# Scores and context of a per-token attention in half tiles, one product to each projection product, with words of q, k and v laid by twos

## What is computed

```python
q = (h @ wq.T + bq).reshape(B, S, H, D)        # H = D = 32; k, v alike
scores = einsum('bshd,bstd->bsht', q, k) / sqrt(D)
probs = softmax(scores, axis=-1)
context = einsum('bsht,bstd->bshd', probs, v).reshape(B, S, E)
x = x + context(layernorm(x))
x = x + ffn(layernorm(x), nf4(w1), nf4(w2), nf4(w3))
```

## Time and profile before

| | us |
|---|---|
| median of 3 runs | 2002.74 |
| lowest, highest | 2000.63, 2002.87 |
| profiled execution: span | 2002.1 |
| PE busy | 1957.2 (98%) |
| DVE busy | 1785.3 (89%) |
| ACT busy | 1456.2 (73%) |
| POOL busy | 1190.3 (59%) |

### The profile page before, as it was taken

How to read it: one execution, slowest core, us unless ns; L and a number is a source line. 1 busy time by engine, 2 the same in 40 slices (tenths; PEclk the granted TensorE clock), 3 DMA queues, 4 the chain that set the end, 5 groups by cost and what they waited for, 6 DMA issues and landing times. The chain is left out here.

```text
span 2002.1 us, 30892 instructions
## 1 busy us (share of the span) xinstructions
PE 1957.2 (98%) x10444; PEld 1072.7 (54%) x10444; DVE 1785.3 (89%) x1789; ACT 1456.2 (73%) x1592; POOL 1190.3 (59%) x714
## 2 busy tenths in 40 slices
PE   6899999999999989999999999999999999999998
PEld 5578777777775434444444444444444444444443
DVE  6788988989878899999999999999999999989982
ACT  7242424233365889989899898998989989898883
...
GB/s 305 90 94 159 143 166 158 136 167 142 127 133 159 220 100 63 42 55 51 52 53 49 55 42 58 47 56 49 43 62 42 63 42 47 58 43 58 38 27 179
DMA packets 253419, 183.77 MB, mean 92 GB/s; under 512 B 177457, under 2 KB 220465, under 8 KB 253361
## 3 DMA queue, kind: packets, MB, share of 16 engines
...
## 5 line engine op out<-in xcount | busy, mean ns | idle before, releaser
L1593 DVE SCALAR_TENSOR_TENSOR bank<-signs,bank 128x1024 f32<-128x1024 int8 (+2 forms) x761 | 926.5, 1217 | 53.9 <-ACT signs L1457 25.9
L1457 ACT ACTIVATE signs<-w_nat,compare_bias 128x1024 int8<-128x1024 f32 (+2 forms) x896 | 959.3, 1133 | 4.2 <-DVE step_part L1591 1.4
L1764 PE MATMUL bank<-x2T_hi,w12T_hi 128*128 128x512 f16 x1376 | 521.5, 379 | 2.1 <-DVE w_nat L1610 1.3
L1765 PE MATMUL bank<-x2T_lo,w12T_hi 128*128 128x512 f16 x1376 | 521.5, 379 | 0.0
L1766 PE MATMUL bank<-x2T_hi,w12T_lo 128*128 128x512 f16 x1376 | 521.5, 379 | 0.0
L985 PE MATMUL bank<-wT_hi,xT_hi 128*128 128x512 f16 x768 | 294.0, 383 | 2.5 <-PEq L324 2.5
L985 PE MATMUL bank<-wT_hi,xT_lo 128*128 128x512 f16 x768 | 294.3, 383 | 0.0
L1791 PE MATMUL bank<-w3T_hi,hT_hi 128*128 128x512 f16 x672 | 255.5, 380 | 9.1 <-DMA w3T_lo<-half 6.3
L1792 PE MATMUL bank<-w3T_lo,hT_hi 128*128 128x512 f16 x672 | 255.4, 380 | 0.0
L1793 PE MATMUL bank<-w3T_hi,hT_lo 128*128 128x512 f16 x672 | 255.2, 380 | 0.0
L1383 POOL TENSOR_TENSOR acc<-acc,hidden 128x512 f32<-128x512 f32 x176 | 221.1, 1271 | 39.4 <-ACT hidden L1506 38.6
(11 more groups left out here) (142 smaller groups left out, 2719.5 us busy)
## 6 DMA issues: line engine op xcount, KB each, us to landing
...
```

The lines of the kernel that those rows point to most:

```text
L1457: nc.scalar.activation(signs[0:rows, ring(v, k), 0:cols], w_nat[0:rows, v % SLOTS, 0:cols], ACT.Sign, scale=COMPARE[SUMMED[k]][0], bias=co ...
L1593: V.scalar_tensor_tensor(to, part, HALF_STEP[SUMMED[k]], before, ALU.mult, ALU.add).then_inc(sign_used, 1)
L1764: nc.tensor.matmul(dst, hi, x2T_hi[:, toks, c], start=c == 0, stop=False)
L1765: nc.tensor.matmul(dst, hi, x2T_lo[:, toks, c], start=False, stop=False)
```

## The change

Four things change together.

1. PE: each of the 32 matmuls of q is followed by one score product, each of the 16 of k's second half by one product of the context's first half, each of the 16 of v's first half by one of its second half.
2. Scores, row maximum, subtraction, exponential, turn, placing and weighing work on halves of 16 positions, a PSUM bank each, with a semaphore count per half. `weigh` and `flip_context` move from the start of the next step (the tail, for tile 14) to the end of the same one. Row maxima and what follows move ahead of q's second evacuation on DVE. The residual moves to the head of POOL's step. ACT's `turn_low2` moves behind the placing of q. The tail's score products keep their places among the early sums, and so do its context products.
3. `qT`, `kT`, `vT` lie as [128, 16, 32, 2]: the turns write two neighbouring words, then step. PE reads kT and vT at every second word.
4. v's dimensions and heads change places: wv's rows are loaded in another order (rows of 4 KB as before), v's bias goes through `qT` and a POOL copy in the first block, and the weighed context and its turn use pairs, too; POOL's add undoes it.

```diff
+                by_dim = w_qkv[2].rearrange("(h t a) e -> t a h e", h=HEADS, a=P // QUAD)
+                for k in range(LOADS):
+                    sp.dma_start(w_raw[2][:, k], by_dim[k]).then_inc(w_in[2][k], 16)
...
+                for m in (2, 0, 1):
+                    to = bias[:, m] if m < 2 else qT[:].rearrange("p t h u -> p (t h u)")
+                    sp.dma_start(to, b_qkv[m].rearrange("(o n) -> o n", o=1).to_broadcast([P, E])).then_inc(bias_in[m // 2], 16)
...
+                pool.wait_ge(bias_in[1], 16)
+                nc.gpsimd.tensor_copy(bias[:, 2].rearrange("p (d h) -> p h d", h=HEADS),
+                                      qT[:].rearrange("p t h u -> p (t h u)").rearrange("p (h d) -> p h d", d=HD)).then_inc(bias_turned, 1)
...
-        kT = sb("kT", [P, QUAD, HEADS])
-        vT = sb("vT", [P, QUAD, HD])
+        kT = sb("kT", [P, QUAD // 2, HEADS, 2])
+        vT = sb("vT", [P, QUAD // 2, HD, 2])
...
+                if end:
+                    residual(n - 2)
...
-                    residual(n - 2)
...
+                rows = x_res[:].rearrange("p (h u d) -> p h u d", u=2, d=HD)
+                nc.gpsimd.tensor_tensor(rows, rows, flipped[:].rearrange("p (h d u) -> p h u d", d=HD, u=2), ALU.add).then_inc(res_done, 1)
...
-                if end:
-                    weigh(n - 2)
                 if attend:
-
                     evacuate(n - 1, 1 - u, it, 2, 1)
+                    turn_v(n)
                 if normalize:
                     norm_stats(dve, n + 1, 1 - u, (n + 1) // 2 + 1 if it is None else it + 2 + u)
-                if end:
-                    flip_context(n - 2)
-                if attend:
-                    turn_v(n)
-                if normalize:
-                    norm_apply(dve, n + 1, 1 - u)
-                look()
                 if end:
                     moments2(n - 2)
...
                 if project:
                     evacuate(n, u, it, 0, 0)
+                if attend:
+                    center(n, 0)
+                if normalize:
+                    norm_apply(dve, n + 1, 1 - u)
+                if attend:
+                    flip_probs(n, 0, end)
+                look()
+                if end:
+                    norm2(n - 2)
+                if attend:
+                    center(n, 1)
+                if project:
                     evacuate(n, u, it, 0, 1)
                 if feed:
                     next(feed)
-                if attend:
-                    center(n)
-                    if feed:
-                        next(feed)
-                if end:
-                    norm2(n - 2)
                 if normalize:
                     split_lo(dve, n + 1, xT_lo[:, 1 - u], xT_hi[:, 1 - u], x_hi_done, x_lo_done)
                 if attend:
-                    flip_probs(n, end)
-                    sum_rows()
-                look()
+                    flip_probs(n, 1, end)
                 if project:
                     dve.wait_ge(evacuated, 6 * n + 2)
                     if not (it is None and n == 0):
                         dve.wait_ge(q_placed, n)
-                    nc.vector.transpose(qT[:].rearrange("p t h -> p h t"),
+                    nc.vector.transpose(qT[:].rearrange("p t h u -> p h t u"),
                                         qkv[:, 0].rearrange("p (h d) -> p h d", d=HD)).then_inc(q_ready, 1)
+                if feed:
...
+                if attend:
+                    sum_rows()
                 look()
                 if project:
                     evacuate(n, u, it, 1, 0)
                 look()
+                if attend:
+                    weigh(n - 1, 0)
                 if project:
                     evacuate(n, u, it, 1, 1)
                     dve.wait_ge(evacuated, 6 * n + 4)
-                    nc.vector.transpose(kT[:].rearrange("p t h -> p h t"),
+                    nc.vector.transpose(kT[:].rearrange("p t h u -> p h t u"),
...
                 look()
                 if project:
                     evacuate(n, u, it, 2, 0)
+                look()
+                if attend:
+                    weigh(n - 1, 1)
+                    flip_context(n - 1)
                 look()
...
-            def weigh(n):
-                dve.wait_ge(context_done, n + 1)
+            def weigh(n, half):
+                part = slice(half * HALF, (half + 1) * HALF)
+                dve.wait_ge(context_done, 2 * n + half + 1)
                 seq.wait(dve)
-                nc.vector.tensor_tensor(probs[:], context, inv_sum[:].unsqueeze(2).to_broadcast([P, QUAD, HD]),
+                nc.vector.tensor_tensor(probs[:].rearrange("p t h -> p (t h)").rearrange("p (d t u) -> p t d u", t=QUAD, u=2)[:, part],
+                                        context[:, part].rearrange("p t (d u) -> p t d u", u=2),
+                                        inv_sum[:, part].unsqueeze(2).unsqueeze(3).to_broadcast([P, HALF, HD // 2, 2]),
                                         ALU.mult).then_inc(ctx_read, 1)
 
             def flip_context(n):
-                dve.wait_ge(ctx_read, n + 1)
-                nc.vector.transpose(flipped[:].rearrange("p (h d) -> p d h", d=HD),
-                                    probs[:].rearrange("p t d -> p d t")).then_inc(ctx_ready, 1)
+                dve.wait_ge(ctx_read, 2 * n + 2)
+                nc.vector.transpose(flipped[:].rearrange("p (h d u) -> p d h u", d=HD, u=2),
+                                    probs[:].rearrange("p t h -> p (t h)").rearrange("p (d t u) -> p d u t", t=QUAD, u=2)).then_inc(ctx_ready, 1)
...
                 dve.wait_ge(evacuated, 6 * n)
-                nc.vector.transpose(vT[:].rearrange("p t d -> p d t"),
-                                    qkv[:, 0].rearrange("p (h d) -> p d h", d=HD)).then_inc(v_ready, 1)
+                nc.vector.transpose(vT[:].rearrange("p t d u -> p d t u"),
+                                    qkv[:, 0].rearrange("p (d h) -> p d h", h=HEADS)).then_inc(v_ready, 1)
...
+            def center(n, half):
+
+                part = slice(half * HALF, (half + 1) * HALF)
+                dve.wait_ge(scores_done, 2 * n + half - 1)
+                seq.mark(nc.vector.tensor_reduce(row_max[:, part], scores[:, part], AX.X, ALU.max))
                 seq.wait(dve)
-                nc.vector.tensor_tensor(probs[:], scores, row_max[:].unsqueeze(2).to_broadcast([P, QUAD, HEADS]),
+                nc.vector.tensor_tensor(probs[:, part], scores[:, part], row_max[:, part].unsqueeze(2).to_broadcast([P, HALF, HEADS]),
                                         ALU.subtract).then_inc(centered, 1)
...
+                if end and half == 0:
                     dve.wait_ge(res_done, n - 1)
...
-                weigh(T - 2)
                 evacuate(T - 1, 1, None, 2, 1)
                 next(feed)
-                flip_context(T - 2)
...
+                center(T, 0)
+                center(T, 1)
+                next(feed)
+                flip_probs(T, 0, True)
+                flip_probs(T, 1, True)
...
+                if attend:
+                    exponential(n, 0)
+                    place_probs(n, 0, end)
...
                 if attend:
-                    exponential(n)
+                    exponential(n, 1)
                 if end:
                     halve2(n - 2)
                     turn_high2(act, n - 2)
                 if attend:
-                    place_probs(n, end)
+                    place_probs(n, 1, end)
                 if feed:
                     next(feed)
-                if end:
-                    turn_low2(act, n - 2)
                 if project:
                     act.wait_ge(q_ready, n + 1)
                     if attend:
...
-                    place(q_diag, qT[:].rearrange("p t h -> p (t h)"), q_placed)
+                    place(q_diag, qT[:].rearrange("p t h u -> p t u h"), q_placed)
+                if end:
+                    turn_low2(act, n - 2)
...
                 if end:
-                    act.wait_ge(context_done, n - 1)
+                    act.wait_ge(context_done, 2 * n + half - 3)
                 else:
                     act.wait_ge(diag_zero, 2)
-                place(p_diag, flipped[:], p_placed)
+                part = slice(half * HALF, (half + 1) * HALF)
+                place(p_diag[:, part], flipped[:].rearrange("p (t u h) -> p t u h", u=2, h=HEADS)[:, half * HALF // 2:(half + 1) * HALF // 2], p_placed)
...
-                    skip = len(passes) if late else len(passes) * 2 // 3 if with_lo else len(passes) // 2
-                    slots = 2 * len(passes) - skip
                     for j, (x, w) in enumerate(passes):
                         ins = nc.tensor.matmul(to, x, w, start=j == 0, stop=j == len(passes) - 1)
                         if j == len(passes) - 1:
                             ins.then_inc(projected, 1)
-                        slot = h * len(passes) + j - skip
-                        if between and slot >= 0:
```

(18 more changed lines are left out.)

82 lines of the change are left out of this document (38 added, 44 removed).

## The result

The changed kernel takes 2016.71 us (median of 7 runs, 2006.62 to 2021.6), the kernel before, on the same chip, 2000.63 (7 runs, 1999.46 to 2004.12). The ratio is **1.0065, 95% interval [1.0047, 1.0083]**: slower by 0.65%, where 1954.3 us had been forecast. The profiled execution took 2010.74 us with a span of 2008.9. It is one of the faster ones: the runs of the changed kernel lie 15 us apart, those of the kernel before 5.

A forecast was written before the change was run, and what follows sets the result against it. The loop was taken to run at PE's rate, with DVE 2.8 us behind. Gains of 27.7 (loop), 8.7 (step 15) and 12.0 (tail) summed to 48.4 us, giving 1954.3 us; range 1950 to 1959 at 0.50, wider 1945 to 1972.

The forecast's parts named there:

- Loop, PE: Tile steps 1 to 14 on PE: 30.64 us a step instead of 32.62, a gain of 27.7 us in all.
- Loop, DVE: DVE in a loop step: halving adds 1.0 us, turns at 1.24 to 1.3 us each save 3.1; 27.8 of 30.6 us busy.
- Loop, the new deadlines: Work on halves in a loop step is ready at least 2 us before PE needs it; SP's loads keep their order.
- Rival 4: Loop: turns not shortened, DVE becomes the bound, PE stalls at half clock, about 2120 us; or products cost more; chance 0.05.
- First steps: Start and step 0: wv's loads move the same bytes in 4 KB rows; effect 0, with -0.5 to +3 us.
- Step 15: Last tile step: no long placing stall, then PE waits for POOL's second diagonal; 34.8 us instead of 43.48, gain 8.7.
- Tail: Stretch up to the feed-forward: no wait for `p_diag`, DVE next to bound; 42 us instead of 53.95, gain 12.0.
- rival 1: Tail: PE's clock stays at half through the 32 score products after idling, 9 us longer, time 1963; chance 0.22.
- rival 2: Only the loop gains; the tail finds other waits and step 15 stalls as before; 1975 us; chance 0.10, whole or part.

The follow-up runs named there:

- both_mended: Changed kernel with each wv load issued as four of 32 rows, and the loop's low-half x2 DMA transpose issued after v's first-half evacuation; 1972.15 us, ratio 0.9854.
- before_wv_by_dim: The kernel before with only the changed kernel's eight wv loads, v's columns then in the wrong order; 2029.07 us, ratio 1.0130.
- wv_four_loads: Changed kernel with each of the eight wv loads issued as four of 32 rows, same rows to same places; 1990.38 us, ratio 0.9929.

## Why the prediction was wrong

*Loop, PE.* Right: 30.64 us a step in eight of 14 of the changed kernel and in all 14 once the meeting of transfers was taken away, in nine kernels; 27.6 for 27.7.

*Loop, DVE.* Right: 1.20 to 1.25 us a turn, and DVE busy 26.1 us a step (364.98 in 14 steps of both_mended) for 27.8. Of the 1.7 too much 1.0 is the start from one tile with 29.87 us, where the 14 steps had 28.9 on average (404.41 in 14). The Trainium skill ("SBUF — State Buffer", Door 1: The DMA port swizzle), of which no row before could tell, says that two accesses to a 16-byte line are enough for full rate, and these rows agree.

*Loop, the new deadlines.* **This step failed**, at its last sentence, "SP's loads keep their order". They do, on SP. But it checked only engines, with 2 us to spare each, and not what a chain that runs 3 us earlier in the step does on the DMA engines: the transpose, issued on ACT's queue, now comes within 1.6 us of three loads. That is 15.9 us in the profiled execution; taking it away is worth 13.9 by the medians (2016.71 less 2002.77), the feed-forward's new stops included. Rival 4 had PE stalling behind a late DVE in the loop, but with slow turns as the cause; no rival had a transfer. Nor is its lateness of 2 us a limit for the clock: a wait of 2.38 us for `p_diag` in step 15 of both_mended left it at 1.00, where one of 2.25 in the kernel before was followed by half clock (0.50 from 618 to 632 us).

*First steps.* **This failed**, and it is the largest error: "wv's loads move the same bytes in rows of 4 KB" priced bytes and row length and took the rate for given. It cost 28.0 us of the span; 26.8 in before_wv_by_dim and 26.3 in wv_four_loads, by medians. The POOL copy, to which the bound of +3 was given, took 1.97 us and held up nothing. By an estimate from the same rule of the Trainium skill ("DMA: Bandwidth & Descriptors", "Why a DMA increments its semaphore by 16 and not by 1"), the 8 x 512 KB would have been put at a quarter of the 407 GB/s of before, 41 us for 10, and the start could not have been 0.

*Step 15.* The mechanism was right, the term mis-sized: 6.0 for 8.7. PE had no long stall for `p_diag` (1.8 us) and then waited 3.8 us up to 599.18, POOL's second diagonal having ended at 599.08 (the row names DVE's evacuation, done at 598.85). The forecast had DVE's look at the scales, and with it POOL's row, 3.5 us earlier; the all-reduce came 12.6 us after the step's start (574.29 less 561.73) for 14.5 before, so 1.9, and 1.0 went in a wait for the third weight tile's load. In both_mended that wait is 2.2 us and the sums start 38.4 us after the step's start.

*Tail.* Right as a length, 11.5 for 12.0. The early sums did start at half clock, as forecast, and it lasted into the first of the score products (602.16), but was over by 603.51, where rival 1 had all 32 products at half clock; it didn't come. Wrong as a gain: "the feed-forward behind 642.92 isn't touched, and I take it to start earlier by whatever is gained ahead of it". **That step failed too.** DVE and ACT, which prepare its weights, were taken for a stage's neighbours, though the tail had DVE at 45.18 of 53.95 us. Of the 20.7 us of step 15 and the tail 9.4 are left at the end of the changed kernel and 3 at the end of both_mended, where 5.4 more go in the waits that came with the late transpose. In size this is nearest to the forecast's rival 2, "only the loop gains", 1975; both_mended took 1972.15.

The sum by what was measured in the profiled execution: +28.0 - 11.7 - 6.0 - 11.5 + 8.1 = +6.9 by rounded rows, against -48.4. The medians lie 16.1 us apart and the profiled executions only 6.8 (2008.9 less 2002.1). The rest may be longer meetings of transfers in other executions; no trace of them was taken, and it isn't shown.
